# A mixer and mixture-of-experts block: expert output products with stationary split weights

## The chip, the cores and the metric

The kernel runs on one core of one Trainium2 chip. The time is the device time of one launch in microseconds (us); the median of three runs before the change is 928.83 us (924.88 to 929.36). The core has five engines that run their own instruction streams: TensorE (PE, with weight loads listed as PEld), VectorE (DVE), ScalarE (ACT), GpSimd (POOL) and the DMA queue that SyncE (SP) fills. They wait for each other by semaphores.

## The reference, cut to what matters

The mixer branch is an mLSTM block: an up projection to 512 features (x_mlstm and z), a causal convolution over 4 taps with swish, gated attention of 4 heads of width 64 with running maxima, a per-head normalisation, the product with swish(z), and a down projection. What follows it is the part that the change touches most:

```python
y = x + (mixer branch)                     # per token, 128 features; 8 sequences of 1024 tokens
x = layernorm(y)
g = sigmoid(xf @ gate_w.T)                 # 16 experts
topv, topi = top_k(g, 4);  wn = topv / sum(topv)
combine = zeros_like(g) with wn at topi
hin, vin = einsum('td,edh->eth', xf, e_win), einsum('td,edh->eth', xf, e_vin)    # 16 experts of width 64
h = silu(hin) * vin * combine.T[:, :, None]
routed = einsum('eth,ehd->td', h, e_wout)
shared = silu(xf @ ws_in) * (xf @ vs_in) @ ws_out                                # width 128
out = layernorm(x + shared + routed)
```

Inputs and outputs are float32. The mixer branch multiplies its heads by swish(z) just before the down projection.

## The kernel before

**Two stages.** In the first stage the kernel goes through 8 sequences in halves of 512 tokens: transposes, up projection, convolution (DVE), swish (ACT). The convolved values go to a DRAM scratch `xact_scratch` (`store_xact`, L369 to L371, 512 KB a half), and swish(z) of all tokens stays on chip in `silu_z` (L661). A scan over gates follows. In the second stage 16 groups of 512 tokens go through attention and experts.

**The loop of the second stage.** `groups` (L316) runs `mix(0, None)`, then `mix(g, g - 1)` for g = 1 to 15, then `ffn(15)`: attention of group g beside the experts of group g - 1. The order of each engine is written by hand. Each `mix` is a list of slots. In slot j TensorE does `ffn_slot(f, j)` (L1383) and then pieces of attention that the table `PE_SLOT` (L1445) puts there: chunks C 0 to 3 in slots 0 to 3, the head transposes H in slot 6, the down projection D in slots 8 and 9. Index j = 0 is the shared expert, j = 1 to 8 are pairs of routed experts (two of width 64 fill 128 partitions).

**One slot of the experts.** `ffn_in` (L1339) forms hin (bank 4) and vin (bank 5), each by three products of 512 columns: inputs and weights are split in a high part and a low remainder in the type float32r, and high x high, low weight x high and high weight x low are summed. ACT takes silu of bank 4 into `s_in` (L742). DVE multiplies with bank 5 into `h1` (L1079). `combine_rows` (L1362) spreads the combine weights of the pair over 128 partitions of bank 6 with a bfloat16 product of 0/1 rows (`pair_rows`) and combine weights in three bfloat16 parts. DVE multiplies `h1` with bank 6 into `h2` (L1083). `ffn_out` (L1370) then multiplies h by the pair's output weights in plain float32: four products with 128 tokens each as the stationary operand, added in bank 7 over all j, which gives tokens on partitions at once. `ffn_sum` (L1085) adds Y, and the layer norm follows.

**What sets the order.** hin of slot j waits until silu of slot j - 1 has emptied bank 4, vin of slot j until `h1` of slot j - 1 has emptied bank 5. On ACT silu stands alone in a slot, apart from copies of attention. POOL forms the decay arguments of the next group (`args`, L524), which wait for the broadcast of running maxima `max_b` from DRAM; the decayed state `kept` (L560); the product of skip and convolution `mixed` (L566); and powers for the norms. SP issues the loads of the next group behind waits (L443 to L459), one after the other.

## Time and profile before

| | before |
|---|---|
| median of 3 runs | 928.83 us |
| the profiled execution | 932.63 us, its span 930.9 us |
| PE busy | 823.6 us (88%) |
| PE weight loads | 641.0 us (69%) |
| DVE busy | 668.9 us (72%) |
| ACT busy | 360.8 us (39%) |
| POOL busy | 371.1 us (40%) |
| DMA | 65.78 MB, 71 GB/s over the span |
| mean granted clock of TensorE | 0.953 |

The span is the time from the first to the last instruction. Busy times count an engine's instructions, not its waits. The ends of matmuls are modelled and include the pipeline, so the distance from one start to the next says what a product costs TensorE. The granted clock is in parts of full speed: 1.00 is 2.4 GHz, 0.50 is 1.2 GHz. One turn of the second stage (a `mix` with g and f) begins with the transposes of Y (L1330); the views below are of one turn in the middle, from 515.08 us to 561.2 us.

### The profile page before, as it was taken

How to read it: one execution, taken by the hardware profiler on the slowest of the kernel's cores; microseconds unless marked ns; L12 is line 12 of the kernel's file. 1: busy time of each engine (PE TensorE's matmuls, PEld its weight loads, DVE VectorE, ACT ScalarE, POOL GpSimd, SP SyncE). 2: the span in 40 equal slices, each digit the busy share in tenths (PEclk: the TensorE clock that was granted, in tenths of full speed). 3: DMA queues.
4: the chain of work that ended last, by engine and by line, in shares of the span. 5: the costliest groups of instructions: out<-in, count | busy, mean ns of one | idle time of the engine just before them, and what ended most of it. 6: DMA issues, size and time to landing. Idle time of an engine off the chain costs nothing.

```text
span 930.9 us, 17559 instructions
## 1 busy us (share of the span) xinstructions
PE 823.6 (88%) x5719; PEld 641.0 (69%) x5719; DVE 668.9 (72%) x1756; ACT 360.8 (39%) x618; POOL 371.1 (40%) x372
## 2 busy tenths in 40 slices
PE   6979846599998999999999998999899999999976
PEld 5657525477777777777777776777777777777754
DVE  4899923566778677778777778677867777778654
ACT  4758721223333333434333434343434343433121
POOL 5040008442636253536353636253625353534200
PEclk8979976789999999999999999999999999999979
DMA  4745425210403040404040403040304040400000
GB/s 112 209 142 184 152 108 144 80 34 1 124 0 124 0 124 0 124 0 124 0 124 0 124 0 124 0 124 0 124 0 124 0 124 0 124 0 23 1 12 11
DMA packets 51231, 65.78 MB, mean 71 GB/s; under 512 B 9968, under 2 KB 36744, under 8 KB 49160
## 3 DMA queue, kind: packets, MB, share of 16 engines
q1 hardware_dynamic: 51208, 65.47, 23.5%
q8 instruction: 15, 0.25, 0.1%
q14 instruction: 8, 0.07, 0.0%
HBM read 48.42 MB, written 17.04 MB: 70 GB/s over the span
## 4 chain that ended last, share of the span: by engine, by line
PE 45%; DVE 19%; issue 15%; DMA 10%; POOL 5%; SPq 3%; ACT 2%; DVEq 1%; POOLq 1%; ACTq 0%
PE bank L1378 12%; DMA max_b<-max_scratch 8%; PE bank L1348 5%; PE bank L1352 5%; PE bank L1349 5%; DVE acc L821 4%; PE bank L1368 4%; PE bank L1321 3%; DVE st L967 3%; PE bank L1297 2%; DVE out_sb L979 2%; DVE Y L979 2%; PE bank L1295 2%; PE bank L1302 1%; POOL D L541 1%
## 5 line engine op out<-in xcount | busy, mean ns | idle before, releaser
L742 ACT ACTIVATE s_in<-bank 128x512 f32<-128x512 f32 x144 | 85.9, 596 | 198.0 <-PE bank L1352 197.2
L1378 PE MATMUL bank<-ewout,h 128*128 128x128 f32 x1024 | 146.5, 286 | 0.0
L1378 PEld LDWEIGHTS bank<-ewout,h 128*128 128x128 f32 x1024 | 123.9, 191 | 25.3 <-issue 25.3
L1079 DVE TENSOR_TENSOR h<-s_in,bank 128x512 f32<-128x512 f32 x144 | 98.1, 682 | 59.6 <-PE bank L1352 51.9
L545 POOL TENSOR_TENSOR rs<-ve,half 128x4 f32<-128x4 f32 x32 | 32.6, 1018 | 270.1 <-DVE ve L975 270.1
L1348 PE MATMUL bank<-yT_hi,in_hi 128*128 128x512 f32 x288 | 128.1, 445 | 8.4 <-DVE h L1079 8.3
L1352 PE MATMUL bank<-yT_lo,in_hi 128*128 128x512 f32 x288 | 115.5, 401 | 0.0
L1349 PE MATMUL bank<-yT_hi,in_lo 128*128 128x512 f32 x288 | 114.4, 397 | 0.0
L1083 DVE TENSOR_TENSOR h<-h,bank 128x512 f32<-128x512 f32 x128 | 87.2, 682 | 19.8 <-PE bank L1368 19.8
L531 POOL TENSOR_TENSOR D<-a_tok,max_b 128x512 f32<-128x512 f32 x64 | 65.4, 1042 | 71.2 <-DMA max_b<-max_scratch 70.3
L929 DVE TENSOR_TENSOR state<-kept,bank 64x130 f32<-64x130 f32 x128 | 36.6, 286 | 72.7 <-POOL kept L560 37.4
L609 ACT ACTIVATE u_sb<-bank 128x260 f32<-128x260 f32 x64 | 24.8, 387 | 147.2 <-PE bank L1297 147.2
L1295 PE MATMUL bank<-state,qs 128*128 128x130 f32 x256 | 56.2, 302 | 28.6 <-issue 14.5
L1297 PE MATMUL bank<-vals,C 128*128 128x65 f32 x512 | 72.7, 266 | 0.0
L821 DVE SCALAR_TENSOR_TENSOR acc<-xm,vecs,acc 128x512 f32<-128x512 f32 x96 | 72.3, 820 | 0.0
L573 POOL TENSOR_TENSOR r_h<-var_h,half 128x8 f32<-128x8 f32 x32 | 52.9, 1653 | 42.6 <-DVE var_h L949 41.5
L1348 PEld LDWEIGHTS bank<-yT_hi,in_hi 128*128 128x128 f32 x288 | 55.4, 193 | 20.9 <-DVE h L1079 14.9
L1297 PEld LDWEIGHTS bank<-vals,C 128*128 128x128 f32 x512 | 69.2, 196 | 0.0
L560 POOL TENSOR_TENSOR kept<-state,decay 128x260 f32<-128x260 f32 x64 | 39.8, 622 | 71.6 <-DVE state L929 71.6
L1295 PEld LDWEIGHTS bank<-state,qs 128*128 128x128 f32 x256 | 41.3, 197 | 37.4 <-issue 34.1
L1352 PEld LDWEIGHTS bank<-yT_lo,in_hi 128*128 128x128 f32 x288 | 54.9, 191 | 12.6
L1349 PEld LDWEIGHTS bank<-yT_hi,in_lo 128*128 128x128 f32 x288 | 55.6, 193 | 5.5
(189 smaller groups left out, 1623.8 us busy)
## 6 DMA issues: line engine op xcount, KB each, us to landing
max_b<-max_scratch SPq DMA_DIRECT2D x16, 1024.0 KB, 8.2
xact_scratch<-xact SPq DMA_DIRECT2D x16, 512.0 KB, 3.1
xa<-xact_scratch SPq DMA_DIRECT2D x16, 512.0 KB, 7.0
inter_w<-inter_scratch SPq DMA_DIRECT2D x32, 256.0 KB, 6.7
x_in<-in_L_attn_x_dram SPq DMA_DIRECT2D x16, 256.0 KB, 3.8
xt_scratch<-x_t SPq DMA_DIRECT2D x16, 256.0 KB, 3.8
xT<-xt_scratch SPq DMA_DIRECT2D x16, 256.0 KB, 8.6
x_res<-in_L_attn_x_dram SPq DMA_DIRECT2D x16, 256.0 KB, 3.0
```

What stands on the lines that cost most here:

```text
L531: pool.tensor_tensor(D[:, kp, par], a_g.rearrange("p k (s two) -> p two k s", two=2)[:, par, 2 * kp:2 * kp + 2] .unsqueeze(3).to_broadcast ...
L573: pool.tensor_tensor(r_h[:, c].rearrange("p k h -> p (k h)"), var_h[:, c].rearrange("p k h -> p (k h)"), half[:, 0:2 * NH], ALU.pow).then_ ...
L742: act.activation(s_in[:, j % 2], bank[4][:], ACT.Silu).then_inc(silu_done, 1)
L821: i = dve.scalar_tensor_tensor(a, src, vecs[:, p, t:t + 1], a, ALU.mult, ALU.add)
L1079: dve.tensor_tensor(dst[:, j % 2], s_in[:, j % 2], bank[5][:], ALU.mult).then_inc(h1_done, 1)
L1083: dve.tensor_tensor(h2[:, (j - 1) % 2], h1[:, (j - 1) % 2], bank[6][:], ALU.mult).then_inc(h2_done, 1)
L1295: pe.matmul(o, qs[:, p, c], state[:, p], start=True, stop=False, skip_group_check=True)
L1297: i = pe.matmul(o[:, par * DV:(par + 1) * DV], C[:, par, kk, p], vals[:, k, 2 * p + par], start=False, stop=True, skip_group_check=True)
L1348: pe.matmul(o, in_hi[:, m, j], yT_hi[:], start=True, stop=False)
L1349: pe.matmul(o, in_lo[:, m, j], yT_hi[:], start=False, stop=False)
L1352: pe.matmul(o, in_hi[:, m, j], yT_lo[:], start=False, stop=True).then_inc(done, 1)
L1378: i = pe.matmul(bank[7][:, k * P:(k + 1) * P], h2[:, j % 2, k * P:(k + 1) * P], w, start=(j == k == 0), stop=(j == NJ), skip_group_check=True)
```

## The change

**Output products.** The output weights are split in high and low parts (`out_hi`, `out_lo`, made once on POOL) and are now the stationary operand; the 512 tokens of h are the moving one. h is split as well: ACT copies h2 to a rounded `h_hi` (`hidden_high`), POOL subtracts to get `h_lo` (`hidden_low`). Three products of 512 columns per j take the place of four float32 products of 128. The result has features on partitions; so at a group's end ACT copies bank 7 to `oT` and TensorE transposes it back in four steps into bank 4 (`out_tokens`).

**Combine weights.** They are split in two float32r parts, the spreading product is float32r, and it stands between hin and vin from slot 3 on.

**Order.** h2, h_hi and h_lo have three buffers. DVE multiplies by combine weights ahead of the slot's other product. On ACT the copy to `h_hi` of slot j - 1 stands ahead of silu of slot j (from slot 3). `mixed` goes from POOL to ACT in slot 1. POOL's differences and masks are spread over the turn.

**z in memory.** swish(z) is written into `xact` and stored with the convolved values (1024 KB a half), and loaded for each group (`load_z`).

```diff
-    xact_d = nc.dram_tensor("xact_scratch", [NG, P, NP * G], F32).ap()
+    xact_d = nc.dram_tensor("xact_scratch", [NG, P, 2 * NP * G], F32).ap()
...
-        pair_rows = sb("pair_rows", [3 * NX, NJ, P], BF16)
+        pair_rows = sb("pair_rows", [P, NJ, P], F32R)
...
-        ewout = sb("ewout", [P, NJ, E])
-        wsout = sb("wsout", [P, P])
+        out_hi = sb("out_hi", [P, NJ + 1, E], F32R)
+        out_lo = sb("out_lo", [P, NJ + 1, E], F32R)
...
-        comb3 = sb("comb3", [P, NC, P // NX, NX], BF16)
-        combT = sb("combT", [3 * NX, G], BF16)
+        comb2 = sb("comb2", [P, NC, 2 * NX], F32R)
+        combT = sb("combT", [P, G], F32R)
         s_in = sb("s_in", [P, 2, G])
         h1 = sb("h1", [P, 2, G])
-        h2 = sb("h2", [P, 2, G])
+        h2 = sb("h2", [P, 3, G])
+        h_hi = sb("h_hi", [P, 3, G], F32R)
+        h_lo = sb("h_lo", [P, 3, G], F32R)
+        oT = sb("oT", [P, G])
...
+            def load_z(g):
+                sp.dma_start(silu_z[:], xact_d[g].rearrange("p (s t) -> p s t", t=G)[:, NP:]).then_inc(z_in, 16)
...
                     load_xa(g + 1)
+                    for p in range(NP):
+                        sp.wait_ge(hs_done[p], g + 1)
+                    load_z(g + 1)
...
+            def hidden_low(f, j):
+
+                if f is None:
+                    return
+                pool.wait_ge(h_hi_done, nth(f, NJ + 1, j))
+                if j >= 3:
+                    pool.wait_ge(out_lo_mm, nth(f, NJ + 1, j - 3))
+                else:
+                    prev(pool, out_lo_mm, f, NJ + 1)
+                pool.tensor_tensor(h_lo[:, j % 3], h2[:, j % 3], h_hi[:, j % 3].bitcast(F32), ALU.subtract
+                                   ).then_inc(h_lo_done, 1)
...
+                keep_state(0)
+                keep_state(1)
+                hidden_low(f, 0)
+                if more:
+                    arg_differences(g + 1, 0, 0)
+                    arg_differences(g + 1, 0, 1)
+                keep_state(2)
+                hidden_low(f, 1)
+                if more:
+                    arg_mask(g + 1, 0, 0)
+                    arg_mask(g + 1, 0, 1)
+                keep_state(3)
+                hidden_low(f, 2)
+                if more:
+                    arg_differences(g + 1, 1, 0)
+                    arg_differences(g + 1, 1, 1)
+                hidden_low(f, 3)
+                normalised(0)
+                hidden_low(f, 4)
+                normalised(1)
+                hidden_low(f, 5)
+                if more:
+                    arg_mask(g + 1, 1, 0)
+                    arg_mask(g + 1, 1, 1)
+                for j in range(6, NJ + 1):
+                    hidden_low(f, j)
...
                         act.wait_ge(up_mm[f], b * 2 * NP + NP + p + 1)
-                        act.activation(silu_z[:, p, bass.ds(b * S + f * G, G)], bank[3 + p][:], ACT.Silu
-                                       ).then_inc(up_out[f], 1)
+                        act.activation(xact[:, f, NP + p], bank[3 + p][:], ACT.Silu).then_inc(up_out[f], 1)
...
+                    if j == 1:
+                        act.wait_ge(xa_in, 16 * (g + 1))
+                        prev(act, down_mm, g)
+                        for p in range(NP):
+                            act.activation(mixed[:, p], xa[:, p], ACT.Copy, scale=vecs[:, p, VS:VS + 1]
+                                           ).then_inc(skip_done, 1)
...
                 if not last:
-                    decays(g + 1)
+                    decays(g + 1, 0, 2)
+                if f is not None:
+                    hidden_high(f, NJ)
+                if not last:
+                    decays(g + 1, 2, 4)
+                if f is not None:
+                    out_copy(f)
                 if not last:
...
 
+            def hidden_high(f, j):
+
+                if j:
+                    act.wait_ge(h2_done, nth(f, NJ, j - 1))
+                else:
+                    act.wait_ge(h1_done, nth(f, NJ + 1, 0))
+                if j >= 3:
+                    act.wait_ge(out_hi_mm, nth(f, NJ + 1, j - 3))
+                    act.wait_ge(h_lo_done, nth(f, NJ + 1, j - 3))
+                else:
+                    prev(act, out_hi_mm, f, NJ + 1)
+                    prev(act, h_lo_done, f, NJ + 1)
+                copy(h_hi[:, j % 3], h2[:, j % 3]).then_inc(h_hi_done, 1)
+
+            def out_copy(f):
+                act.wait_ge(out_lo_mm, (f + 1) * (NJ + 1))
+                prev(act, o_mm, f)
+                copy(oT[:], bank[7][:]).then_inc(oT_done, 1)
...
             def ffn_slot(f, j):
                 if j == 2:
                     act.wait_ge(combT_mm, f + 1)
-                    copy(combT[:], bank[6][0:3 * NX, 0:G // 2].bitcast(BF16)).then_inc(combT_out, 1)
+                    prev(act, bc_mm, f, NJ)
+                    copy(combT[0:2 * NX], bank[6][0:2 * NX, :]).then_inc(combT_out, 1)
+                if j:
+                    hidden_high(f, j - 1) if j != 2 else None
                 act.wait_ge(hin_mm, nth(f, NJ + 1, j))
                 if j >= 2:
                     act.wait_ge(h1_done, nth(f, NJ + 1, j - 2))
                 act.activation(s_in[:, j % 2], bank[4][:], ACT.Silu).then_inc(silu_done, 1)
+                if j == 2:
+                    hidden_high(f, 1)
 
...
-                    after(12)
-                    dve.tensor_tensor(comb_r[:, 1], comb_r[:, 0], comb3[:, :, 1], ALU.subtract).then_inc(route, 1)
-                    after(13)
-                    dve.tensor_copy(comb3[:, :, 2], comb_r[:, 1]).then_inc(route, 1)
+                    dve.tensor_tensor(comb2[:, :, NX:], comb[:], comb2[:, :, 0:NX].bitcast(F32), ALU.subtract
+                                      ).then_inc(route, 1)
+
+            def hidden(f, j):
+
+                dve.wait_ge(silu_done, nth(f, NJ + 1, j))
+                dve.wait_ge(vin_mm, nth(f, NJ + 1, j))
+                if j >= 3:
+                    dve.wait_ge(h2_done, nth(f, NJ, j - 3))
+                if j == 0:
+                    prev(dve, h_lo_done, f, NJ + 1)
+                    dst = h2[:, 0]
+                else:
+                    dst = h1[:, j % 2]
+                dve.tensor_tensor(dst, s_in[:, j % 2], bank[5][:], ALU.mult).then_inc(h1_done, 1)
+
+            def weigh_hidden(f, j):
+                dve.wait_ge(h1_done, nth(f, NJ + 1, j))
+                dve.wait_ge(bc_mm, nth(f, NJ, j - 1))
+                if j >= 3:
+                    dve.wait_ge(h_lo_done, nth(f, NJ + 1, j - 3))
+                else:
+                    prev(dve, h_lo_done, f, NJ + 1)
+                dve.tensor_tensor(h2[:, j % 3], h1[:, j % 2], bank[6][:], ALU.mult).then_inc(h2_done, 1)
...
-                    dve.wait_ge(h1_done, nth(f, NJ + 1, j - 1))
-                    dve.wait_ge(bc_mm, nth(f, NJ, j - 2))
-                    dve.tensor_tensor(h2[:, (j - 1) % 2], h1[:, (j - 1) % 2], bank[6][:], ALU.mult).then_inc(h2_done, 1)
+                    weigh_hidden(f, j - 1)
+                if j <= NJ and j != 2:
+                    hidden(f, j)
...
 
                 for m, (done, free) in enumerate(((hin_mm, silu_done), (vin_mm, h1_done))):
+                    if m and j >= 3:
+                        combine_rows(f, j - 1)
                     if j:
                         pe.wait_ge(free, nth(f, NJ + 1, j - 1))
...
-
+            def ffn_out_high(f, j):
+                pe.wait_ge(h_hi_done, nth(f, NJ + 1, j))
+                if j == 0:
+                    pe.wait_ge(yT_hi_done, f + 1)
+                    pe.wait_ge(yT_lo_done, f + 1)
+                pe.matmul(bank[7][:], out_hi[:, j], h_hi[:, j % 3], start=(j == 0), stop=False)
+                pe.matmul(bank[7][:], out_lo[:, j], h_hi[:, j % 3], start=False, stop=False).then_inc(out_hi_mm, 1)
+
+            def ffn_out_low(f, j):
+                pe.wait_ge(h_lo_done, nth(f, NJ + 1, j))
+                pe.matmul(bank[7][:], out_hi[:, j], h_lo[:, j % 3], start=False, stop=(j == NJ)).then_inc(out_lo_mm, 1)
+
+            def out_tokens(f):
+                pe.wait_ge(oT_done, f + 1)
+                pe.wait_ge(silu_done, (f + 1) * (NJ + 1))
                 for k in range(NC):
-                    i = pe.matmul(bank[7][:, k * P:(k + 1) * P], h2[:, j % 2, k * P:(k + 1) * P], w,
-                                  start=(j == k == 0), stop=(j == NJ), skip_group_check=True)
-                if j == NJ:
-                    i.then_inc(o_mm, 1)
+                    i = pe.transpose(bank[4][:, k * P:(k + 1) * P], oT[:, k * P:(k + 1) * P], ident[:])
+                i.then_inc(o_mm, 1)
...
-                if 2 <= j <= NJ + 1:
+                if j == 2 or j == NJ + 1:
                     combine_rows(f, j - 1)
-                if j >= 2:
-                    ffn_out(f, j - 2)
+                if 2 <= j <= NJ + 2:
+                    ffn_out_high(f, j - 2)
+                if j >= 3:
+                    ffn_out_low(f, j - 3)
 
...
-                if not (isinstance(g, int) and g == NG - 1):
-                    mix_front(g + 1)
+                last = isinstance(g, int) and g == NG - 1
+                if not last:
+                    mix_keys(g + 1)
+                if f is not None:
+                    out_tokens(f)
+                if not last:
+                    mix_values(g + 1)
```

The first place is ScalarE in slots 5 to 8 and at the end of a turn. `s_in` is silu, `h_hi` the rounded copy, `D` the decay exponentials of the next group. Before:

```order
L742 ACTIVATE s_in<-bank 128x512
L694 ISA
L696 ACT_TABLE_LOAD
L696 ACTIVATE D<-D 128x512
L694 REGISTER_ALU
L696 ACTIVATE D<-D 128x512
```

After:

```order
L669 ACTIVATE h_hi<-h 128x512
L834 REGISTER_ALU
L837 ACTIVATE s_in<-bank 128x512
L755 ISA
L757 ACT_TABLE_LOAD
L757 ACTIVATE D<-D 128x512
L755 REGISTER_ALU
L757 ACTIVATE D<-D 128x512
L811 REGISTER_ALU
L669 ACTIVATE h_hi<-h 128x512
```

A copy now stands ahead of each silu, and the last copy stands behind the table load and two exponentials.

The second place is TensorE in slot 5. `in_hi` and `in_lo` are input weights, `combT` the combine weights. Before:

```order
L1348 MATMUL bank<-yT_hi,in_hi 128x512
L1349 MATMUL bank<-yT_hi,in_lo 128x512
L1352 MATMUL bank<-yT_lo,in_hi 128x512
L1348 MATMUL bank<-yT_hi,in_hi 128x512
L1349 MATMUL bank<-yT_hi,in_lo 128x512
L1352 MATMUL bank<-yT_lo,in_hi 128x512
L1368 MATMUL bank<-combT,pair_rows 128x512
L1378 MATMUL bank<-ewout,h 128x128 x4
```

After:

```order
L1462 MATMUL bank<-yT_hi,in_hi 128x512
L1463 MATMUL bank<-yT_hi,in_lo 128x512
L1466 MATMUL bank<-yT_lo,in_hi 128x512
L1481 MATMUL bank<-combT,pair_rows 128x512
L1462 MATMUL bank<-yT_hi,in_hi 128x512
L1463 MATMUL bank<-yT_hi,in_lo 128x512
L1466 MATMUL bank<-yT_lo,in_hi 128x512
L1488 MATMUL bank<-h_hi,out_hi 128x512
L1489 MATMUL bank<-h_hi,out_lo 128x512
L1493 MATMUL bank<-h_lo,out_hi 128x512
```

The product with `combT` moved in front of vin's three, and three output products stand where four did.

The third place is VectorE in slots 4 and 5: products by combine weights (L1186), by bank 5 (L1177), and head_scale between them. After:

```order
L1186 TENSOR_TENSOR h<-h,bank 128x512
L1177 TENSOR_TENSOR h<-s_in,bank 128x512
L1036 SCALAR_TENSOR_TENSOR nrm<-u_sb 128x8
L1038 SCALAR_TENSOR_TENSOR nrm<-nrm,floor_tok 128x8
L1041 SCALAR_TENSOR_TENSOR nrm<-nrm 128x8
L1044 TENSOR_REDUCE ssq<-sq 128x8
L1048 SCALAR_TENSOR_TENSOR var_h<-ssq,nrm 128x8
L1186 TENSOR_TENSOR h<-h,bank 128x512
L1177 TENSOR_TENSOR h<-s_in,bank 128x512
```

The product by combine weights of slot 5 stands behind all of head_scale; before, only the product by bank 5 did.

## Rows read from the trace of the kernel before

**Rows 1.** Windows: us, busy by engine (instructions), granted clock, DMA share, GB/s.
```profile
184.30:887.00 702.70, 660.04 (x4322) 520.25 (x4322) 524.32 (x1481) 260.15 (x425) 315.00 (x305) 0.99 0.19 56
...
515.08:561.20 46.12, 44.04 (x290) 34.59 (x290) 34.97 (x100) 17.92 (x29) 21.69 (x22) 1.00 0.21 63
```
**Rows 2.** Chain that ended last, in the turn: start, us, what.
```profile
521.34 7.95 DMA max_b<-max_scratch
...
537.10 0.69 DVE h L1079
537.84 0.50 PE bank L1348
```
**Rows 3.** Timeline of TensorE, slots 5, 6, 8 and keys: start, us, instruction.
```profile
539.96 0.48 PE L1348 MATMUL bank<-yT_hi,in_hi 128*128 128x512 f32 x1
...
542.76 0.47 PE L1348 MATMUL bank<-yT_hi,in_hi 128*128 128x512 f32 x1
543.08 0.39 PE L1349 MATMUL bank<-yT_hi,in_lo 128*128 128x512 f32 x1
...
543.99 0.40 PE L1352 MATMUL bank<-yT_lo,in_hi 128*128 128x512 f32 x1
544.32 0.39 PE L1368 MATMUL bank<-combT,pair_rows 48*128 48x512 bf16 x1
544.64 1.16 PE L1378 MATMUL bank<-ewout,h 128*128 128x128 f32 x8
...
549.21 0.47 PE L1348 MATMUL bank<-yT_hi,in_hi 128*128 128x512 f32 x1
...
556.16 1.88 PE L1240 MATMUL bank<-xa,w_key 128*128 128x512 f32 x4
```
**Rows 4.** Timeline of ScalarE in the same turn.
```profile
536.60 0.63 ACT L717 ACTIVATE sq<-u_sb 128x512 f32<-128x512 f32 x1
...
550.18 0.60 ACT L742 ACTIVATE s_in<-bank 128x512 f32<-128x512 f32 x1 [2.19 <-PE bank L1352]
550.80 1.28 ACT L696 ACT_TABLE_LOAD   x1
552.09 2.19 ACT L696 ACTIVATE D<-D 128x512 f32<-128x512 f32 x4
```
**Rows 5.** Timeline of VectorE in the same turn.
```profile
533.38 0.59 DVE L929 TENSOR_TENSOR state<-kept,bank 64x130 f32<-64x130 f32 x2 [3.20 <-POOL kept L560]
534.00 0.30 DVE L937 SCALAR_TENSOR_TENSOR nrm<-u_sb 128x8 f32<-128x8 f32 x1
...
540.12 0.16 DVE L937 SCALAR_TENSOR_TENSOR nrm<-u_sb 128x8 f32<-128x8 f32 x1
...
541.69 0.69 DVE L1079 TENSOR_TENSOR h<-s_in,bank 128x512 f32<-128x512 f32 x1
...
546.35 1.41 DVE L956 SCALAR_TENSOR_TENSOR mixed<-bank,vecs,mixed 128x512 f32<-128x512 f32 x2 [0.58 <-PE bank L1311]
547.67 1.28 DVE L960 TENSOR_TENSOR mixed<-mixed,silu_z 128x512 f32<-128x512 f32 x2
...
557.81 0.68 DVE L1087 TENSOR_TENSOR z<-bank,Y 128x512 f32<-128x512 f32 x1
```
**Rows 6.** GpSimd by line and form: busy us, mean ns, idle before.
```profile
L531 POOL TENSOR_TENSOR D<-a_tok,max_b 128x512 f32<-128x512 f32 x64 | 65.4, 1042 | 71.2 <-DMA max_b<-max_scratch 70.3 <-DVE C L912 1.0
L573 POOL TENSOR_TENSOR r_h<-var_h,half 128x8 f32<-128x8 f32 x32 | 52.9, 1653 | 42.6 <-DVE var_h L949 41.5
...
L551 POOL TENSOR_TENSOR qs<-xa,inter_w 128x1024 f32<-128x1024 f32 x16 | 37.7, 2358 | 2.0 <-DMA inter_w<-inter_scratch 2.0
```
**Rows 7.** Windows of the first stage.
```profile
92.00:102.00 10.00, 10.00 (x120) 6.99 (x120) 10.00 (x18) 8.44 (x17) 0.00 (x0) 1.00 0.62 206
```
**Rows 8.** Timeline of TensorE, a wait in an early turn.
```profile
199.67 0.40 PE L1358 MATMUL bank<-ident_bf,comb 128*128 128x128 bf16 x4 [2.19 <-DVE comb L1069]
```
**Rows 9.** Window of 1 us shortly after that wait.
```profile
201.00:202.00 1.00, 1.00 (x4) 0.21 (x2) 0.58 (x2) 0.46 (x1) 1.00 (x2) 0.51 0.00 0
```

More of the change, by code:

```diff
@@ L111, in mixer_moe_block @@
         w_val = sb("w_val", [P, INNER])
-        silu_z = sb("silu_z", [P, NP, B * S])
         a_tok = sb("a_tok", [P, B, HALVES, NC, NH])
@@ L213, in mixer_moe_block @@
         xa = sb("xa", [P, NP, G])
+        silu_z = sb("silu_z", [P, NP, G])
         xT2 = sb("xT2", [P, G])
@@ L436, in _ @@
                                  ).then_inc(decay_in, 16)
+            load_z(0)
             sp.dma_start(x_res[:], x_g[0]).then_inc(x_res_in, 16)
@@ L501, in _ @@
             i.then_inc(blocks_made, 1)
-            halves = pair_rows[:].rearrange("r j (t m) -> r j t m", t=P // HX)
-            for part in range(3):
+            halves = pair_f[:].rearrange("r j (t m) -> r j t m", t=P // HX)
+            for part in range(2):
                 pool.affine_select(out=halves, in_=halves, compare_op=ALU.not_equal, fill=1.0, base=-NX * part,
@@ L522, in _, with arg_differences @@
             masked = pool.to_reg(NEG)
[L524 to L526 removed]
+            def arg_differences(g, kp, par):
+                if kp == par == 0:
                     pool.wait_ge(max_in, 16 * (g + 1))
                 a_g = a_tok[:].rearrange("p b f k h -> p (b f) k h")[:, bass.ds(g, 1)].rearrange("p g k h -> p (g k) h")
[L529 to L542 removed]
@@ new lines, in arg_differences, with arg_mask @@
+                prev(pool, C_done[kp][par], g)
+                pool.tensor_tensor(
+                    D[:, kp, par],
+                    a_g.rearrange("p k (s two) -> p two k s", two=2)[:, par, 2 * kp:2 * kp + 2]
+                    .unsqueeze(3).to_broadcast([P, 2, NP, P]),
+                    max_b[:].rearrange("p (s two) (k t) -> p two k s t", two=2, k=NC)[:, par, 2 * kp:2 * kp + 2],
+                    ALU.subtract).then_inc(arg_sub, 1)
+            def arg_mask(g, kp, par):
+                pool.wait_ge(arg_sub, nth(g, 4, 2 * kp + par))
+                alone(pool)
+                d = D[:, kp, par].rearrange("p k s t -> p (k s) t")
+                pool.affine_select(out=d, in_=d, compare_op=ALU.is_ge, fill=masked, base=0,
+                                   pattern=[[0, 2 * NP], [1, P]], channel_multiplier=-1).then_inc(arg_masked, 1)
@@ L554, in mix, with keep_state @@
                 dec = decay[:].rearrange("p s (g k) -> p g k s", k=NC)[:, bass.ds(g, 1)].rearrange("p g k s -> p (g k) s")
-                for k in range(NC):
+                more = not (isinstance(g, int) and g == NG - 1)
+                def keep_state(k):
                     if k:
@@ L561, in mix, with normalised @@
                                        ALU.mult).then_inc(kept_done[k], 1)
-                    if k == 0:
-                        prev(pool, down_mm, g)
-                        alone(pool)
-                    if k < NP:
-                        pool.tensor_scalar(mixed[:, k], xa[:, k], vecs[:, k, VS:VS + 1], None, ALU.mult
-                                           ).then_inc(skip_done, 1)
-                    if k in (1, 2) and not (isinstance(g, int) and g == NG - 1):
-                        args(g + 1, k - 1)
-                for kp in range(2):
+                def normalised(kp):
                     c = slice(2 * kp, 2 * kp + 2)
@@ L582, in mix, with norm_power, ffn @@
                 if f is not None:
-                    ffn(f)
-                if not (isinstance(g, int) and g == NG - 1):
+                    norm_power(f)
+                if more:
                     weigh_queries(g + 1)
-            def ffn(f):
+            def norm_power(f):
                 pool.wait_ge(ve2_done, f + 1)
                 power(rs2[:], ve2[:], rs2_done)
+            def ffn(f):
+                for j in range(NJ + 1):
+                    hidden_low(f, j)
+                norm_power(f)
             pool.wait_ge(back_out, 1)
@@ L689, in mix_front, with decays @@
                      bank[3][:].rearrange("p (q d) -> p q d", d=DH)).then_inc(val_out[0], 1)
-            def decays(g):
-                for q in range(4):
+            def decays(g, first=0, last=4):
+                for q in range(first, last):
                     act.wait_ge(arg_masked, nth(g, 4, q))
@@ L747, in ffn @@
                     ffn_slot(f, j)
+                hidden_high(f, NJ)
+                out_copy(f)
             phase1_xt(0, 0)
@@ L959, in gate_heads @@
                     dve.wait_ge(mixed_done[p], g + 1)
-                    dve.tensor_tensor(mixed[:, p], mixed[:, p], silu_z[:, p, bass.ds(g * G, G)], ALU.mult
+                    dve.tensor_tensor(mixed[:, p], mixed[:, p], silu_z[:, p], ALU.mult
                                       ).then_inc(hs_done[p], 1)
@@ L1398, in mix @@
                     ffn_logits(f)
-                for j in range(NJ + 3):
+                for j in range(NJ + 4):
                     if f is not None:
@@ L1404, in mix @@
                             if arg is not None else head_transposes(g)
-                if not (isinstance(g, int) and g == NG - 1):
-                    mix_front(g + 1)
+                last = isinstance(g, int) and g == NG - 1
[5 more added lines that the diff above has]
+                    mix_values(g + 1)
             def ffn(f):
@@ L1410, in ffn @@
                 ffn_logits(f)
-                for j in range(NJ + 3):
+                for j in range(NJ + 4):
                     ffn_slot(f, j)
+                out_tokens(f)
             mix_keys(0)
@@ L1449 @@
 U_SLOT = {0: 0, 1: 1, 2: 2, 3: 3}
-IDENT = 9
-CONSTS = 14
+IDENT = 7
+CONSTS = 12
 SCAN_DECAY = 10
```

83 lines of the change are left out of this document (33 added, 50 removed).

## The prediction, made before the changed kernel ran

> **What bounds the kernel now.** I read the windows first: of the span of 930.9 us, 702.7 us are the turns from 184.3 to 887 us, and one turn in the middle takes 46.12 us, in which TensorE is busy for 44.04 us at a granted clock of 1.00, which is 2.4 GHz, VectorE for 34.97, ScalarE for 17.92 and GpSimd for 21.69 us [rows 1]. So TensorE bounds most of a turn. The chain of waits shows the exception: from 521.34 us the broadcast of max_b takes 7.95 us, GpSimd then forms differences, masks and kept, VectorE adds the state at 533.38 after waiting 3.20 us for kept [rows 5] and forms h at 537.10, and only from 537.84 on does the chain stay on TensorE [rows 2]. The reader is to see two parts: up to about 537 us memory, GpSimd and VectorE lead, from there TensorE's own work does.
>
> In the second part a slot without attention lasts from 539.96 to 542.76, 2.80 us. Its parts are distances between starts: products of 512 columns follow each other after 0.23 us (four from 543.08 to 543.99), the second of a slot 0.32 after the first; combine rows stand 0.33 after vin's last product and output products 0.32 after them; the output products have the rest, 2.80 - 1.56 - 0.32 = 0.92 us [rows 3]. ScalarE waits 2.19 us for silu in such a slot [rows 4], so it looks free.
>
> **What the change takes from TensorE.** Three output products cost 3 x 0.23 = 0.69 us for 0.92, nine times: -2.1 us in a turn. Combine rows without the switch of types cost 0.23 for some 0.33 + 0.32 - 0.23 = 0.42, eight times: -1.5. Added are four transposes of oT (some 0.7, as four products of 128 tokens take up to 0.92) and dearer ones of combine weights (0.2). The net is -2.7 us in a turn, if all stays bound by TensorE. Routing loses three VectorE instructions of about 0.24, which stand ahead of the transposes in slot 2; those wait for TensorE's own work then, and the time up to kept is set by max_b.
>
> **What it adds is a loop.** Before, hin of slot j waited for silu of slot j - 1 and nothing else came round. Now ScalarE's queue has h_hi of j - 1 ahead of silu of j. With E the end of silu of j - 1: hin starts at E + 0.05; its three products and combine rows bring the latter's start to E + 0.84 (0.05 and 0.32 + 0.23 + 0.23), its end, as records of such products last 0.39, to E + 1.23 [rows 3]; VectorE's product by the weights is done at E + 1.95 (0.68 and 0.04) [rows 5]; the copy to h_hi (as sq, 0.63) starts at E + 2.0, silu some 0.55 behind it, and ends after its 0.60 at E + 3.15 [rows 4]. A slot so lasts at least 3.15 us, where TensorE's ten products need 2.4 and before it took 2.80. What VectorE has between its products now falls into the loop as well: head_scale, 1.5 us, in slot 4 and the gating of the heads, 2.53 us (1.41 and 1.28 less an overlap of 0.16) from 546.35 on, in slot 6 [rows 5].
>
> Now one turn with the clock of the trace, all starts up to max_b as before.
> - Slots 2 and 3: max_b at 529.3 to 529.5, as nothing just ahead of its load on SP moved (load_z goes out earlier, between turns). GpSimd takes two differences of 1.04 [rows 6] and kept, now ahead of the masks, so the state is added from 532.15, 1.2 us sooner than the 533.38 before. Then comes head_scale. It took 3.1 us here (534.00 to 537.10) and 1.57 in slot 4 (540.12 to 541.69) [rows 5], beside a busy and an idle GpSimd; I take 2.6. The product by weights of pair 2 ends at 536.05, h_hi at 536.73, silu of slot 3 at 537.25, and hin of slot 4 starts at 537.30. The 1.2 us won are gone: before, hin of slot 4 was through when vin followed at 537.84.
> - Slot 5: one loop, 540.45. Slot 6: head_scale stands before the product by weights (ends 543.4), hin at 544.65. The head transposes wait for hn. GpSimd has now h_lo of pairs 3 and 4 and two differences in front of two powers of 1.65 and two products of 1.04 [rows 6]; I get 548.1, and hin of slot 7 at 549.05; before it lay a slot of 2.80 ahead of 549.21, at 546.4 [rows 3].
> - Gating holds VectorE until 551.4, then weights, h_hi, silu: hin of slot 8 at 553.3. It was 549.21: 4.1 us late.
> - The tail: silu of slot 8 ends at 556.4. Behind it stand a table load of 1.28 and two exponentials of about 0.53 [rows 4] ahead of the last h_hi, which ends at 559.35; GpSimd's last h_lo (half of 2.36 for a tile of 1024, 1.2 us [rows 6]) at 560.6, keys start at 560.9 (before 556.16 [rows 3]), the copy to oT is hidden beside them, transposes of oT start at 562.6 after keys of 1.72. z starts at 563.35 for 557.81 before [rows 5], and from z to the next turn it is 3.39 us as before (561.20 less 557.81): 566.75.
>
> The turn takes 566.75 - 515.08 = 51.7 us, 5.55 more. For 15 turns: +83 us. Both ends of this cost: with head_scale at 1.57, no wait for hn and the tail's waits half as long I get 49.2, +3.1 a turn or +46; with 3.1 us for head_scale and a second of further queueing on GpSimd 53.2, +7 or +106.
>
> **The rest.** The last group alone has six loops of 0.36 more and a longer end (h_hi 0.63, h_lo 1.2, copy 0.6 and transposes 0.7 in series for a product of 1.1): +4.5. The first stage stores 0.5 MB more in every half of 5.5 us, 95 GB/s on top of 206 at a DMA share of 0.62 [rows 7]; scaled that is a share of 0.9. I take +5, from 0 to +20 us: loads of x then arrive behind longer stores. The last store stands on the way to the second stage: +2. The splits of the output weights lie in GpSimd's idle time in the first stage: 0. The skip product in slot 1 on ScalarE lies beside its waits: 0.
>
> Sum: 932.6 (the profiled execution, span and launch) + 83 + 4.5 + 5 + 2 = 1027. The medians lie 3.8 us lower (928.8), so 1023.
>
> The Trainium skill, "GPSIMD Engine Reference", section "Specifications", says that GpSimd shares its SBUF interfaces with VectorE, with contention for instructions with two SBUF inputs. The gating's second pair (mixed by silu_z) has two such inputs and would meet h_lo there; its 0.68 us each [rows 5] were taken with GpSimd idle. By that page I estimate up to 1.2 us more in a turn, 18 us in all, and 1041; no row here shows that pair beside a busy GpSimd.
>
> **The rivals.**
> - The clock falls. With the walk above TensorE waits some 2.0 us before hin of slot 4, 1.75 in slot 5 and 1.8 in slot 7. In one place before, it waited 2.19 us, and 1.3 us after the end of that wait the granted clock was 0.51 [rows 8, 9]. The 2.1 us of idle time that a middle turn holds in pieces (46.12 - 44.04) left it at 1.00 [rows 1]. If two of the three do this in each turn, with two slots at 0.43 for 0.23 us in four products of the loop (0.8 each), plus the heads, a turn takes 2.4 us more: +36, 1059. Against it: the waits are shorter than 2.19. Chance 0.20.
> - A shorter chain: head_scale short, hn in time, as worked out above: 46 us instead of 83, 986. For it: GpSimd's spans are rough. Chance 0.22.
> - Faster: TensorE's work decides after all, because ScalarE's copies and silu pass each other, that is the loop costs under 2.4 us a slot. Then the -2.7 us apply, 15 times -40, with 8 for the rest: 932.6 - 40 + 8 = 900 less 4, 896. The point from which it decides is a loop of 2.80 us; I see 3.15 from rows that are each firm to 0.05, and the order of the queue is fixed. Chance 0.07.
> - The change does what it says but both effects cancel (loop 2.9, no added waits): within 0.5%. Chance 0.03.
> The forecast has 0.48.
>
> **Range and chances.** The forecast's own ends are 986 and 1050. 8 in 10 is 973 to 1064; it takes in the short chain and the clock. What the measurement can tell from no change is 0.5%, 4.6 us. Faster 0.07, same 0.03, slower 0.90.
>
> **What would show it.** In the new profile: silu of slots 5 to 8 at least 3.1 us apart, its releaser hin but h_hi just ahead of it; in the turns TensorE busy below 85% with idle time ahead of hin that ends with silu; a turn of 50 to 53 us; h_hi of the shared copy at 0.63 us, h_lo near 1.2; idle time before the head transposes ended by hn; keys about 45.8 us after the turn's start, before 41.1. Slots at 2.4 us would refute the loop, a turn below 46 us the whole forecast; a granted clock below 0.95 in the turns would be the first rival.

## The result, and the profile after

The changed kernel takes 1015.88 us (median of 4 runs, 1012.33 to 1017.12), the kernel before beside it 929.1 us: ratio 1.0946, 95% interval 1.0907 to 1.0985. It is slower by 9.5%. The profiled execution has a span of 1015.4 us for 930.9. Ratios here and below leave out executions in a slower state of the chip that any kernel can meet; that was one of e2's, the one that was profiled.

The windows of the kernel after, over its 15 turns and over one in the middle (columns as in [rows 1]):
```profile
192.10:968.80 776.70, 646.76 (x3710) 515.11 (x3711) 524.05 (x1436) 359.13 (x605) 438.76 (x410) 0.97 0.20 60
558.00:609.10 51.10, 42.05 (x249) 33.35 (x249) 34.51 (x97) 24.47 (x41) 29.91 (x29) 1.00 0.24 67
```
TensorE's work in the middle turn fell from 44.04 to 42.05 us, and the turn grew from 46.12 to 51.10: TensorE waits 9 us of it. Each row on TensorE that is shown below with a releaser stands behind such a wait. The page's costliest groups (busy us, mean ns, idle time of the engine just before them and what ended it) name two of the new instructions and the wait:
```profile
L574 POOL TENSOR_TENSOR h_lo<-h,h_hi 128x512 fp32r<-128x512 f32 x144 | 185.3, 1287 | 169.9 <-ACT h_hi L669 149.7
L669 ACT ACTIVATE h_hi<-h 128x512 fp32r<-128x512 f32 x144 | 90.6, 629 | 302.2 <-DVE h L1186 300.7
L1462 PE MATMUL bank<-yT_hi,in_hi 128*128 128x512 f32 x288 | 132.0, 458 | 82.6 <-ACT s_in L837 82.6
```
82.6 us of idle time ahead of hin, over the whole kernel, end with silu (s_in). The loop itself runs from hin of slot 4 (579.25) to hin of slot 5 (582.37). TensorE's rows show it, and where TensorE waits after it in the same turn (hn are the normalised heads that GpSimd makes):
```profile
579.25 0.50 PE L1462 MATMUL bank<-yT_hi,in_hi 128*128 128x512 f32 x1 [1.55 <-ACT s_in L837]
580.05 0.39 PE L1481 MATMUL bank<-combT,pair_rows 128*128 128x512 f32 x1
580.98 0.40 PE L1488 MATMUL bank<-h_hi,out_hi 128*128 128x512 f32 x1
582.37 0.51 PE L1462 MATMUL bank<-yT_hi,in_hi 128*128 128x512 f32 x1 [0.53 <-ACT s_in L837]
586.62 0.50 PE L1462 MATMUL bank<-yT_hi,in_hi 128*128 128x512 f32 x1 [1.65 <-ACT s_in L837]
590.22 1.09 PE L1422 MATMUL bank<-ident,hn 128*128 128x128 f32 x8 [1.00 <-POOL hn L604]
595.52 0.50 PE L1462 MATMUL bank<-yT_hi,in_hi 128*128 128x512 f32 x1 [1.90 <-ACT s_in L837]
601.64 0.50 PE L1488 MATMUL bank<-h_hi,out_hi 128*128 128x512 f32 x1 [0.81 <-ACT h_hi L669]
603.34 1.88 PE L1351 MATMUL bank<-xa,w_key 128*128 128x512 f32 x4
```
then VectorE's product by the weights, and ScalarE's copy and silu:
```profile
580.48 0.69 DVE L1186 TENSOR_TENSOR h<-h,bank 128x512 f32<-128x512 f32 x1
```
```profile
581.20 0.63 ACT L669 ACTIVATE h_hi<-h 128x512 fp32r<-128x512 f32 x1 [0.99 <-DVE h L1186]
581.74 0.58 ACT L837 ACTIVATE s_in<-bank 128x512 f32<-128x512 f32 x1
```
hin starts at 579.25, combine rows at 580.05, the product by the weights at 580.48, the copy at 581.20, silu at 581.74 and the next hin at 582.37: once round is 3.12 us. ScalarE waits (0.99) for VectorE, and silu's input, ready since 580.2 (hin's third product starts at 579.82 and lasts 0.39), waits behind the copy in its queue. In [rows 3] such a slot took 2.80 us.

### The profile page after: what moved, and what is told of

Read it like the earlier page. It is cut to its first block, busy times and chain, and to the rows that moved or that the text cites. A ratio compares the mean times of both kernels' runs of the same rounds, so it can differ in the third digit from the quotient of the medians.

```text
span 1015.4 us, 17232 instructions
## 1 busy us (share of the span) xinstructions
PE 811.5 (80%) x5063; PEld 636.8 (63%) x5063; DVE 672.0 (66%) x1708; ACT 467.0 (46%) x810; POOL 507.0 (50%) x484
## 4 chain that ended last, share of the span: by engine, by line
PE 28%; POOL 20%; issue 17%; DVE 15%; DMA 9%; ACT 7%; SPq 2%; POOLq 1%; DVEq 1%; ACTq 0%
POOL h_lo L574 7%; DMA max_b<-max_scratch 6%; POOL r_h L601 5%; PE bank L1462 3%; POOL D L545 3%; PE bank L1351 3%; PE bank L1466 3%; PE bank L1463 3%; DVE acc L920 3%; DVE h L1186 3%; PE bank L1408 2%; ACT s_in L837 2%; POOL D L556 2%; POOL hn L604 2%; PE bank L1422 2%
## 5 line engine op out<-in xcount | busy, mean ns | idle before, releaser
L574 POOL TENSOR_TENSOR h_lo<-h,h_hi 128x512 fp32r<-128x512 f32 x144 | 185.3, 1287 | 169.9 <-ACT h_hi L669 149.7
L669 ACT ACTIVATE h_hi<-h 128x512 fp32r<-128x512 f32 x144 | 90.6, 629 | 302.2 <-DVE h L1186 300.7
L1462 PE MATMUL bank<-yT_hi,in_hi 128*128 128x512 f32 x288 | 132.0, 458 | 82.6 <-ACT s_in L837 82.6
L1177 DVE TENSOR_TENSOR h<-s_in,bank 128x512 f32<-128x512 f32 x144 | 98.4, 683 | 126.9 <-ACT s_in L837 113.4
L1466 PE MATMUL bank<-yT_lo,in_hi 128*128 128x512 f32 x288 | 119.5, 415 | 0.0
L1463 PE MATMUL bank<-yT_hi,in_lo 128*128 128x512 f32 x288 | 118.8, 413 | 0.0
L1186 DVE TENSOR_TENSOR h<-h,bank 128x512 f32<-128x512 f32 x128 | 87.7, 686 | 31.4 <-PE bank L1481 26.8
L545 POOL TENSOR_TENSOR D<-a_tok,max_b 128x512 f32<-128x512 f32 x64 | 65.5, 1044 | 74.3 <-DMA max_b<-max_scratch 74.3
L1408 PE MATMUL bank<-vals,C 128*128 128x65 f32 x512 | 76.5, 275 | 0.0
L1408 PEld LDWEIGHTS bank<-vals,C 128*128 128x128 f32 x512 | 73.6, 207 | 0.0
L1488 PE MATMUL bank<-h_hi,out_hi 128*128 128x512 f32 x144 | 60.4, 419 | 9.7 <-ACT h_hi L669 9.7
L1493 PE MATMUL bank<-h_lo,out_hi 128*128 128x512 f32 x144 | 60.3, 419 | 6.4 <-POOL h_lo L574 6.4
L1406 PEld LDWEIGHTS bank<-state,qs 128*128 128x128 f32 x256 | 46.0, 207 | 28.2 <-issue 22.7
```

The costliest lines, as they stand in the source:

```text
L545: pool.tensor_tensor(D[:, kp, par], a_g.rearrange("p k (s two) -> p two k s", two=2)[:, par, 2 * kp:2 * kp + 2] .unsqueeze(3).to_broadcast ...
L574: pool.tensor_tensor(h_lo[:, j % 3], h2[:, j % 3], h_hi[:, j % 3].bitcast(F32), ALU.subtract).then_inc(h_lo_done, 1)
L669: return act.activation(dst, src, ACT.Copy)
L1177: dve.tensor_tensor(dst, s_in[:, j % 2], bank[5][:], ALU.mult).then_inc(h1_done, 1)
L1186: dve.tensor_tensor(h2[:, j % 3], h1[:, j % 2], bank[6][:], ALU.mult).then_inc(h2_done, 1)
L1406: pe.matmul(o, qs[:, p, c], state[:, p], start=True, stop=False, skip_group_check=True)
```

## The experiments

Ratios are to runs of the kernel before on the same chip. "A turn" is the distance between the first transposes of Y of the first and the last turn, over 15: 46.9 us before, 51.7 after. The kernels are called e1 to e11 and e123 after the first letters of their labels. "The wait for" something is TensorE's idle time that ends with it, over the whole profiled execution.

**Orders in queues.** Four kernels, three edits (in slot 2 silu already stood first in the changed kernel; 0 and 1 at norm are the two pairs of heads):
```
 ScalarE, slots from 3 on:  - h_hi(j-1); silu(j)      + silu(j); h_hi(j-1)
 ScalarE, end of a turn:    - table, 2 exps, last h_hi, 2 exps  + last h_hi, table, 4 exps
 GpSimd:  - h_lo(3) norm(0) h_lo(4) norm(1)           + norm(0) h_lo(3) norm(1) h_lo(4)
```


> The changed kernel with one edit on ScalarE: from slot 2 on silu of slot j stands ahead of the copy to h_hi of slot j - 1. Theory (the loop silu, hin, combine rows, product by weights, h_hi, silu sets slots 3 to 8): slots 4 and 5 fall from 3.12 and 4.25 us to 2.4 to 2.7, the wait of hin for silu (82.6 us in all) nearly vanishes, and what is left is the wait of the head transposes for hn on GpSimd; a turn falls from 51.1 to about 47.2 us, the time from 1016 to about 958 (940 to 985). Rival (GpSimd's h_lo, 20% of the chain, is the bound): the turn stays within 1 us of 51.1, the time above 1000. Rival (the rounded copies themselves cost, wherever they stand): no change either.

Measured: 978.04 us, ratio 1.056 (1.0505 to 1.0614). The loop is real, but opening it gives back only 36 us of the 87, where 58 were expected. The wait for silu is gone (idle before hin 82.6 to 2.3 us); the wait for hn has grown from 20.7 to 47.7, and ahead of combine rows 19.1 us end with VectorE's product. What a wait for hn does in a turn:
```profile
574.56 1.09 PE L1422 MATMUL bank<-ident,hn 128*128 128x128 f32 x8 [2.82 <-POOL hn L604]
575.96 0.60 PE L1466 MATMUL bank<-yT_lo,in_hi 128*128 128x512 f32 x1
578.92 0.62 PE L1493 MATMUL bank<-h_lo,out_hi 128*128 128x512 f32 x1
579.35 0.43 PE L1462 MATMUL bank<-yT_hi,in_hi 128*128 128x512 f32 x1
```
From 575.96 to 579.35 eight products last 0.60 to 0.63 us and follow each other after 0.43 instead of 0.23. The granted clock of that stretch is 0.50 (1.2 GHz), where it is 1.00 in the 1.4 us of work between the wait's end and it. The eight products cost another 1.6 us.

> The changed kernel with the last copy to h_hi ahead of the table load and the exponentials of the next group. The last product by weights is done at 600.21 us in the trace and its copy starts at 600.98, so the theory gives 0.7 to 0.8 us a turn: 12 us less, about 1004. Rival (the end of a turn waits for GpSimd's h_lo or for VectorE's norms in any case): no change, 1016.

Measured: 1017.73 us, ratio 1.0977 (1.0883 to 1.1071). No difference from the changed kernel can be told: as the rival had it, the last copy's place is worth nothing. What the end of a turn waits for is another thing than the rival named. The wait for the copies h_hi ahead of the output products falls from 9.7 to 2.2 us, and the wait for the copy to oT rises from 1.4 to 8.1: ScalarE now begins the table load behind the last h_hi, and its copy to oT stands behind all four exponentials. In e123 the wait for the copy to oT is 8.1 us too.

> The changed kernel with GpSimd's two head normalisations ahead of h_lo of pairs 3 and 4. TensorE waits 1.00 us for hn in the middle turn (20.7 us in all) while its own work is done at 589.2: the theory gives 1.0 to 1.2 us a turn, 16 us less, about 1000. Rival (h_lo then comes too late for its own product and VectorE's waits for buffers grow): no change or slower.

Measured: 1022.98 us, ratio 1.1054 (1.1001 to 1.1108), 1% slower than the changed kernel; the theory missed. The wait for hn fell as it said, from 20.7 to 5.7 us, but the idle time before hin rose from 82.6 to 98.1. With the loop in place an earlier hn buys nothing.

> The three edits together: silu ahead of the copy, the last copy ahead of the exponentials, head normalisations ahead of h_lo. With the loop gone hn becomes the next wait, so the edits add up to more than their sum: a turn of about 43.5 us, 15 turns 7.6 us shorter, about 902 (885 to 930). If only the single gains add up it is about 930. Rival (h_lo on GpSimd is the bound): above 980.

Measured: 963.9 us, ratio 1.043 (1.0374 to 1.0487). Missed by 60 us: something outside of these orders holds the turn. 38.5 us are still waited for hn.

**Undo the output products**, and with them the places that they asked for: combine rows stand behind vin again, and VectorE's product by bank 5 ahead of the one by the weights. The rest is kept:
```
- pe.matmul(bank[7][:], out_hi[:, j], h_hi ...) and two more, h_hi, h_lo, oT, its transposes
+ for k in range(NC): pe.matmul(bank[7][:, k*P:(k+1)*P], h2[:, j%2, k*P:(k+1)*P], out_w[:, j], ...)
```


> The changed kernel with the output products of the kernel before (h as stationary operand at 4 bytes, no split of h on ScalarE and GpSimd, no transposes of the output, order of the combine rows as before); kept from the change are the combine weights as two float32r parts, z written to memory and read back, the skip product on ScalarE and GpSimd's new order. Theory (the new chain through the split of h is the loss, z in memory costs the first stage 8 us): 936, range 926 to 948, that is some 8 to 13 above the kernel before. Rival (the loss lies in what is kept: z's load, combine weights, GpSimd's order): 965 or more. Rival (the stages cost nothing): 925.

Measured: 872.38 us (868.03 to 874.12), ratio 0.9439 (0.9406 to 0.9471). Far outside of every expectation, and the fastest kernel of this study. So what is kept of the change gains 50 us, and the output products, with the split of h and the two places above, cost some 140. The windows, over 15 turns and over one:
```profile
188.40:832.00 643.60, 623.82 (x4323) 541.47 (x4323) 506.67 (x1436) 279.15 (x455) 269.16 (x275) 0.99 0.24 72
489.68:533.04 43.36, 41.79 (x290) 35.99 (x290) 33.99 (x97) 19.03 (x31) 18.54 (x20) 1.00 0.27 79
```
TensorE is busy 97% of the turns. A slot without attention on TensorE:
```profile
514.50 0.40 PE L1437 MATMUL bank<-yT_lo,in_hi 128*128 128x512 f32 x1
514.74 0.39 PE L1452 MATMUL bank<-combT,pair_rows 128*128 128x512 f32 x1
514.97 1.05 PE L1460 MATMUL bank<-out_w,h 128*128 128x128 f32 x8
515.77 0.48 PE L1433 MATMUL bank<-yT_hi,in_hi 128*128 128x512 f32 x1
```
The four starts lie 0.24, 0.23 and 0.80 us apart. In [rows 3] they were 0.33, 0.32 and some 0.9 with combine rows in bfloat16: the bfloat16 product costs 0.3 us, at its own start, behind it, and in the output products that follow. It also had 48 rows in place of 128; no run tells the type from the rows.

**Early maxima.** On the sync engine the load of max_b is issued when the last differences are made, ahead of the output's store.

> The changed kernel, with one edit on the sync engine: the load of the next group's running maxima (max_b, 7.9 us to land) is issued as soon as the last differences are made, ahead of the store of the output rows and the load of the residual rows, so GpSimd's differences no longer wait for it (4.87 us in one turn of the kernel with all three orders changed). Theory (hin's loop through ScalarE sets the turn, GpSimd's wait is only the next bound): small gain, 1 us in a turn where head transposes wait for hn: 1000, range 992 to 1014. Rival (GpSimd's late start sets the turn): 975 or less.

Measured: 1010.28 us, ratio 1.0951 (1.0926 to 1.0976); the changed kernel had 1.0946. No change, where 1000 us (992 to 1014) were expected. The load does come earlier: GpSimd's wait for max_b falls from 74.3 to 23.9 us, and the wait for hn stays (20.7 and 21.5).

> The kernel with all three orders changed (963.9 earlier) and the early load of the maxima as well. Theory (with silu first, the turn is set by hn, which GpSimd makes late since it has been busy without a gap since the maxima landed): head transposes' wait of 2.2 us in a turn goes, and the slower clock behind it: 2.5 us x 15 = 38: 927, range 915 to 945. Rival (DVE's order or the combine rows are as late, the gain is given back): 955 or more.

Measured: 964.12 us, ratio 1.0446 (1.0422 to 1.0471); without the early load 1.043, where 927 us (915 to 945) were expected. The theory is wrong as it stood: the wait for hn is 38.5 us in both, so GpSimd is not late because the maxima are. It now waits for h_hi instead, and the second pair of differences and two remainders still stand in its queue around hn:
```profile
553.14 1.29 POOL L584 TENSOR_TENSOR h_lo<-h,h_hi 128x512 fp32r<-128x512 f32 x1 [3.70 <-ACT h_hi L679]
557.96 1.30 POOL L584 TENSOR_TENSOR h_lo<-h,h_hi 128x512 fp32r<-128x512 f32 x1 [1.76 <-ACT h_hi L679]
559.21 2.05 POOL L555 TENSOR_TENSOR D<-a_tok,max_b 128x512 f32<-128x512 f32 x2
```


> The kernel before with the early load of the maxima alone. Its differences also started when the maxima landed, 14.4 us into a turn, but hn was not waited for long: 0 to -1 us in a turn, so 0 to -15: the same as before or up to 1.5% faster, estimate 918 where before is 923.

Measured: 945.44 us, ratio 1.0249 (1.022 to 1.0277): slower than before, where the same time or up to 1.5% less was expected. The differences and masks on GpSimd now run beside VectorE's splits of the combine weights:
```profile
530.67 2.04 POOL L541 TENSOR_TENSOR D<-a_tok,max_b 128x512 f32<-128x512 f32 x2
532.67 1.23 POOL L551 TENSOR_SCALAR_AFFINE_SELECT D<-D 128x512 f32<-128x512 f32 x2
```
```profile
531.07 0.69 DVE L1071 CAST comb<-comb 128x64 bf16<-128x64 f32 x1
531.80 0.99 DVE L1073 TENSOR_TENSOR comb_r<-comb 128x64 f32<-128x64 f32 x1
532.83 0.53 DVE L1075 CAST comb<-comb_r 128x64 bf16<-128x64 f32 x1
```
The same three in the kernel before, with GpSimd idle (it waits for max_b):
```profile
525.71 0.20 DVE L1061 CAST comb<-comb 128x64 bf16<-128x64 f32 x1
525.94 0.22 DVE L1063 TENSOR_TENSOR comb_r<-comb 128x64 f32<-128x64 f32 x1
526.20 0.20 DVE L1065 CAST comb<-comb_r 128x64 bf16<-128x64 f32 x1
```
VectorE's three end at 531.76, 532.79 and 533.36, each 0.05 to 0.08 us behind the end of an instruction of GpSimd's (the two differences take 1.04 each and the first mask 0.64: 531.71, 532.71, 533.31). So each is not slowed by a factor but ends when GpSimd's instruction has ended. TensorE's wait for these weights rises from 13.0 to 37.5 us; that is 24.5 us, and the kernel lost 23.

**GpSimd's remainder of h**, left out with and without the three orders. These two kernels leave the low part of h out of the sum and serve only to price it. Waits for h_lo, also those that free buffers of h, became waits for h_hi or for the third product:
```
- pool.tensor_tensor(h_lo, h2, h_hi, subtract)
- pe.matmul(bank[7][:], out_hi[:, j], h_lo[:, j % 3], ...)   + the same with h_hi[:, j % 3]
```


> The kernel with all three orders changed (963.9 and 964.1 with the early maxima), without h_lo: GpSimd makes no remainder of h, and TensorE's third product of a slot reads h_hi again, so TensorE and ScalarE do the same work (the low part of h is left out of the sum). Theory (with silu first GpSimd sets the turn: 9 remainders of 1.29 us make hn late, and the slower clock comes behind that wait): the wait for hn (2.2 us in a turn), for h_lo (0.4) and the slow products behind go: 4 us x 15: 904, range 885 to 925. Rival (the copy h_hi on ScalarE or VectorE's order takes over at once): 945 or more.

> The changed kernel without h_lo, all orders as in it (the low part of h is left out of the sum; TensorE's and ScalarE's work the same). Theory (in this order hin waits for silu, that for h_hi, that for VectorE's product: GpSimd is not in that loop): only the wait for hn (1.0 us) and for h_lo (0.4) go: 1016 - 15 x 1.5 = 994, range 980 to 1008. Rival (GpSimd's remainder is the cause in both orders): 950 or less.

Measured: 904.83 us, ratio 0.976 (0.9679 to 0.9841), and 998.53 us, ratio 1.0751 (1.0647 to 1.0856). Both as the theory had it (904 and 994). The wait for hn before TensorE's transposes, with the three orders, first with the remainder, then without:
```profile
L1420 PE MATMUL bank<-ident,hn 128*128 128x128 f32 x128 | 22.2, 330 | 38.5 <-POOL hn L604 38.5
```
```profile
L1419 PE MATMUL bank<-ident,hn 128*128 128x128 f32 x128 | 18.3, 288 | 6.4 <-POOL hn L603 6.4
```
The wait is 32 us less, and the rest of the 59 us is seen in TensorE's busy time, which falls from 810.3 to 786.5 us for the same instructions; over the turns the granted clock is 0.97 with the remainder and 0.99 without. With the orders of the change and no remainder, hin still waits for silu:
```profile
L1461 PE MATMUL bank<-yT_hi,in_hi 128*128 128x512 f32 x288 | 136.0, 472 | 90.3 <-ACT s_in L836 90.3
```
Ratios to the kernel before, side by side:

| | with h_lo | without h_lo |
|---|---|---|
| orders of the change | 1.095 | 1.075 |
| all three orders changed | 1.043 | 0.976 |

Either edit alone leaves the other as the bound. Alone they are worth 2 and 5 points, together 12.

**One part alone, and the swap without a split.**
```
 e10, on the kernel before: - comb3 (three bf16 parts), pair_rows BF16
                            + comb2 (two float32r parts), pair_rows F32R
 e11, on e4: - four products of 128 columns, h stationary
             + pe.matmul(bank[7][:], out_w[:, j], h2[:, j % 2], ...); oT, its four transposes
```


> The kernel before with one part of the change: combine weights as two float32r parts instead of three bfloat16 ones. Output products, z in on-chip memory, GpSimd's order and the skip product stay as they were. Theory (the gain of 50 us in the kernel with the output products undone is this part: a bfloat16 product between others of 4 bytes takes 0.33 + 0.32 us in place of 0.23 + 0.23, and the output products behind it 0.91 in place of 0.80: 0.30 us x 8 in a turn, and 0.7 us less wait for the combine weights' transposes): 923 - 15 x 3.2 - 3 = 872, range 862 to 885. Rival (the gain is the skip product on ScalarE and GpSimd's order): 900 or more.

Measured: 887.93 us, ratio 0.9591 (0.9511 to 0.9671). The theory holds for most of it, 4.1 of 5.6 points; 872 was too low, and 887.93 lies outside of its range. TensorE's busy time falls from 823.6 to 787.5 us, some 0.3 us for each of the 128 combine rows; the wait for the combine weights falls from 13.0 to 1.9. Its turn is 44.0 us, that of e4 42.9; the rest lies in what e4 has besides (skip product on ScalarE, GpSimd's order, z from memory), which was not taken apart.

> The kernel with the output products undone (872), but with the weights as stationary operand and h at 4 bytes as moving one, in one product of 512 columns in a slot: no split of h on ScalarE or GpSimd; with it come the copy of the output to memory, its four transposes and the wait for them at a turn's end. Theory (the tail costs 1.5 us in a turn, as key products to next Y show: 6.46 against 4.95; a 4-byte product of 512 columns is 0.86 against 0.80 for the four of 128): 872 + 16 x 2.0 = 904, range 888 to 918. Rival (the tail hides, since VectorE's chain to Y is as late anyway): 880 or less.

Measured: 881.55 us, ratio 0.9506 (0.9415 to 0.9596), a turn of 43.5 us against 42.9. The rival is nearer: in this kernel, which has the places of e4 on TensorE and VectorE, output product, copy and transposes in this form cost some 0.6 us in a turn, not 2. The product is one pair of records, 0.86 us to the next start:
```profile
504.87 1.02 PE L1465 MATMUL bank<-h,out_w 128*128 128x512 f32 x2
505.73 0.39 PE L1384 MATMUL bank<-state,qs 128*128 128x130 f32 x2
```
The tail is therefore not what makes the change slow. What parts this kernel from the changed one is the split of h and the places that came with it: combine rows ahead of vin, the product by the weights ahead of the one by bank 5, three buffers. The split takes 0.17 us off this product in a slot, and from 0.951 the ratio goes to 1.095. That the split and not the places alone does it is argued, not shown by a run of its own: the loop goes through the copy that only the split needs, and e1, which moves that copy and leaves the places, opens it. Even with all three orders changed and GpSimd's part left out the split stays behind (0.976): there 17.5 us are waited for the copy to oT, 1.4 here. That kernel still has the changed places, so part of the 0.976 can be theirs.

## Why the prediction was right

The forecast was 1023 us (973 to 1064, slower 0.90); measured 1015.88. Its mechanism, the loop through ScalarE's queue, is what the trace shows. Point by point, in the middle turn from its start:

| step, us | predicted | measured |
|---|---|---|
| maxima landed | 14.3 | 13.4 |
| head_scale beside GpSimd | 2.6 | 2.63 |
| hin of slot 4 | 22.2 | 21.25 |
| once round the loop | 3.15 | 3.12 |
| hin of slot 8 | 38.2 | 37.5 |
| key products | 45.8 | 45.34 |
| whole turn | 51.7 | 51.10 |

- **The loop.** As predicted, link by link, and e1 shows it by undoing it. The head start of 0.9 us comes from max_b, whose load was issued 5.5 us into the turn and not 6.3 as before. The walk keeps it to hin of slot 7 (33.07 for 33.97) and loses 0.2 by slot 8 and 0.2 more by the key products. The 2.6 us for head_scale was a choice between 1.57 and 3.1 that no sum gave; that it hit to 0.03 is in part luck.
- **15 turns.** +73.2 us measured (703.0 to 776.2), +83 predicted. The turn came out 0.57 us shorter than walked, which is 8.6 of the 10 us that are missing; the turns before were on average 0.75 us longer than the one I walked, those after 0.65. The turns of the changed kernel ran at a mean clock of 0.97 for 0.99. Cut into fifteen equal windows they show 0.91 to 1.00, so the rival of a falling clock is there, small, in some turns; the middle one, with waits of 1.55 to 1.90 us, stayed at 1.00.
- **First stage** +7.8 (5 + 2 predicted), **last group** +3.6 (4.5 predicted, though its own terms add up to 4.2): a store of 1 MB of xact landed in 4.9 us, one of 0.5 MB before in 3.1.
- **GpSimd.** h_lo 1.29 us (1.2 predicted). The gating's second pair took 1.41 us where it took 1.28 alone, not up to 1.2 more, because it runs mostly behind GpSimd's masks here. In the kernel with all three orders it meets them and takes 1.98. The page "GPSIMD Engine Reference" of the Trainium skill, section "Specifications", has this contention for VectorE instructions with two inputs in SBUF or in a 2-port perf mode. The trace agrees for two inputs (1.98 for 1.28); the casts above have one input and grow too (0.20 to 0.69), and no run here shows which mode they ran in. By that page I had put up to 18 us on it; the forecast left them out, and nothing like it came.
- **What TensorE gains** was mis-sized in its parts. I gave 2.1 us to the output products (0.92 to 0.69) and 1.5 to combine rows. Against e4 the output products in this form gain only 0.80 - 0.69 = 0.11 us in a slot, 1.0 in a turn; the other 0.12 is a cost of the bfloat16 neighbour, which combine rows alone take away. The net was to be -2.7 us in a turn; TensorE's busy time in the middle turn fell by 2.0. In the changed kernel all of it is hidden under the loop, so the sum did not notice.
- **The range.** Its upper end for the forecast alone, 1050, does not follow from the terms: 106 in place of 83 gives 1046. Nothing hangs on it.
- **What I did not see** is how much lay behind the loop. My rival "faster" (896, if ScalarE's copies and silu pass each other) is refuted in its reason: e1 is that kernel, and it takes 978, because hn is next. Had silu stood first, that sum would have been my forecast, and wrong by 80 us.

What stays open: which of the three kept edits makes e4 1.5 points faster than e10; what fills the 1.4 us in a turn between e8 and e11 beside the wait for oT, which is 1.0 of it; and what the new places of combine rows and of VectorE's products cost without the split.

## What to carry to other kernels

- An instruction of 0.6 us on an engine that was 39% busy before can set the time: draw the loop through the queues before moving a copy there, and ask which instruction of the next step is behind it. When the loop is opened, look for the second engine that is loaded by the same edit; here each hid the other, and only a two-by-two of runs showed 12 points where single ones gave 2 and 5.
- Run a mixed change in parts. This one has a part that gains 4.1% and another that costs 14 points; together they read as "9.5% slower".
- A transfer that arrives late can be what keeps two engines from meeting on chip memory; moving it up lost 2.5%.

## What the runs showed of the hardware

- One bfloat16 product of 48 rows among 4-byte ones costs 0.3 us more than a float32r product of 128 rows and the same 512 columns (before against e4): its own start +0.10, the next instruction's +0.09, and +0.1 in the products after it.
- In e7 three short instructions of VectorE between tiles in on-chip memory, started while GpSimd worked, ended 0.05 to 0.08 us behind GpSimd's instruction (0.20 became 0.69, 0.22 became 0.99). VectorE's products that read a PSUM bank took 0.69 us beside a busy and an idle GpSimd.
- In e1, 1.4 us after an idle time of 2.82 us had ended, TensorE's granted clock stood at 0.50 and its products of 512 columns 0.43 us apart in place of 0.23, from 575.96 to 579.35.
